# Two raw tiles for the rotary stage of a fused attention block, and a new order of the work around them

## The reference

```
x = x + attn(cond(x, subject, cond_weights, fside), WA, bA, WB, bB, WC, bC, WUQ, WUK, WUV, WZ, bZ)
x = x + ffn(lora(x, W, A, Bm, scalings, adapter), Wg, bg, W1, W2)

cond:  out = einsum('bct,bcd->bdt', x, cond_weights[subject]) + bias
attn:  h = x @ WA + bA;  kv_lat, q_lat = split(h)
       kRt = rope(h @ WB + bB)              # 64 rotary key features, shared by the heads
       qRt = rope(h @ WC + bC)              # 64 rotary query features for each of 16 heads
       q, k, v = q_lat @ WUQ, kv_lat @ WUK, kv_lat @ WUV
       scores = [q, qRt] . [k, kRt] / sqrt(192), causal;  softmax;  out = (attn @ v) @ WZ + bZ
rope:  x * cos + (pairs of x swapped, one of each negated) * sin
ffn:   4 experts, top 2, capacity 1024, gelu(x @ W1) @ W2, added to the tokens taken
```

## Time and profile before

| | |
|---|---|
| median of three runs | 1929.16 us |
| the profiled execution, its own time | 1927.72 us |
| its span, first to last instruction | 1925.6 us |
| mean granted TensorE clock | 0.985 |
| TensorE busy | 1825.1 us, 95% of the span |
| VectorE, ScalarE, GpSimd busy | 922.9, 627.2 and 705.7 us |
| attention's eight groups | about 46 to 967 us of the span |

### The profile page before, as it was taken

How to read it: one execution, slowest core, us unless ns; L and a number is a source line. 1 busy time by engine, 2 the same in 40 slices (tenths; PEclk the granted TensorE clock), 3 DMA queues, 4 the chain that set the end, 5 groups by cost and what they waited for, 6 DMA issues and landing times. The chain is left out here.

```text
span 1925.6 us, 29419 instructions
## 1 busy us (share of the span) xinstructions
PE 1825.1 (95%) x10664; PEld 1418.1 (74%) x10664; DVE 922.9 (48%) x1581; ACT 627.2 (33%) x1088; POOL 705.7 (37%) x525
## 2 busy tenths in 40 slices
PE   6899999999999999999999997999999999999996
PEld 4577676777767677677777776888888888888884
DVE  4565656556565665656433683242424232333321
ACT  4333333333333333333223112333333333333331
POOL 1232223223221222322100033565757575757563
PEclk9999999999999999999999998999999999999998
DMA  7000101010010100102033115033304230422011
GB/s 259 23 1 17 51 6 62 1 42 26 17 51 6 62 1 29 39 17 61 17 120 110 50 66 191 22 71 106 85 0 109 87 65 0 131 87 44 6 16 22
DMA packets 68588, 104.81 MB, mean 54 GB/s; under 512 B 12304, under 2 KB 29456, under 8 KB 68496
## 3 DMA queue, kind: packets, MB, share of 16 engines
q1 hardware_dynamic: 53568, 76.92, 12.2%
q0 software_dynamic: 7200, 16.78, 4.9%
q10 hardware_dynamic: 7728, 9.71, 1.4%
HBM read 78.23 MB, written 25.17 MB: 54 GB/s over the span
## 5 line engine op out<-in xcount | busy, mean ns | idle before, releaser
L1861 DVE CAST hh<-hid 128x512 fp32r<-128x512 f32 x128 | 92.6, 723 | 453.3 <-ACT hid L1806 453.3
L1731 POOL TENSOR_TENSOR w1l<-w_raw,w1h 128x512 fp32r<-128x512 f32 x112 | 185.3, 1654 | 153.4 <-ACT w1h L1798 153.3
L441 POOL TENSOR_TENSOR prob<-prob,rinv 128x512 f32<-128x512 f32 x64 | 66.7, 1043 | 460.1 <-DVE rinv L700 460.1
L95 PE MATMUL bank_o<-Mh,mix_h 128*128 128x512 f32 x512 | 211.6, 413 | 2.3 <-DVE mix_l L671 1.4
L95 PE MATMUL e_h<-xh,w1h 128*128 (+1 forms) x512 | 203.5, 397 | 5.6 <-POOL w1l L1731 5.6
L97 PE MATMUL e_h<-xh,w1l 128*128 (+1 forms) x512 | 202.7, 396 | 0.0
L96 PE MATMUL e_h<-xl,w1h 128*128 (+1 forms) x512 | 202.7, 396 | 0.0
L97 PE MATMUL bank_o<-Mh,mix_l 128*128 128x512 f32 x512 | 202.6, 396 | 0.0
L96 PE MATMUL bank_o<-Ml,mix_h 128*128 128x512 f32 x512 | 202.2, 395 | 0.0
L95 PE MATMUL e_y<-w2h,hh 128*128 128x512 f32 x512 | 201.2, 393 | 0.0
L96 PE MATMUL e_y<-w2l,hh 128*128 128x512 f32 x512 | 200.6, 392 | 0.0
(11 more groups left out here) (303 smaller groups left out, 3486.3 us busy)
## 6 DMA issues: line engine op xcount, KB each, us to landing
w_raw<-in_W_dram SPq DMA_DIRECT2D x56, 512.0 KB, 4.2
stage<-in_x_dram SPq DMA_DIRECT2D x8, 1024.0 KB, 6.3
x_res<-in_x_dram SPq DMA_DIRECT2D x32, 256.0 KB, 3.2
out_dram<-x_res SPq DMA_DIRECT2D x32, 256.0 KB, 2.0
flat_dram<-flat_sb ACTq DMA_DIRECT2D x32, 256.0 KB, 2.0
rows<-out_dram SPq DMA_DIRECT2D x4, 1024.0 KB, 5.4
stage<-in_W_dram SPq DMA_DIRECT2D x8, 512.0 KB, 5.6
x_res<-out_dram SPq DMA_DIRECT2D x3, 1024.0 KB, 5.2
```

What stands on the lines that cost most here:

```text
L95: nc.tensor.matmul(out, ah, bh, start=start and n == 0, stop=False)
L441: nc.gpsimd.tensor_tensor(prob[:, i % 2, :, :], prob[:, i % 2, :, :], rinv[:, :].unsqueeze(2).to_broadcast([P, HB, C]), ALU.mult).then_inc ...
L1731: nc.gpsimd.tensor_tensor(w1l[:, k, :, :], w1_at(pair, chunk), w1h[:, k, :, :].bitcast(F32), ALU.subtract).then_inc(S["w1_lo"], 1)
L1861: nc.vector.tensor_copy(hh[:, k, :], hid[:, k, :]).then_inc(S["h_hi"], 1)
```

## The change

`rope_raw` becomes two tiles used in turn: the keys take tile 0, query rotation u takes tile (u + 1) mod 2, and `q_raw` waits for the swap and the cosine product of the rotation before the last. On ScalarE, `prob_transposed(g, 1)` goes ahead of `exps(g, 2)`, the first `q_raw` of the second half ahead of `exps(g, 3)`, and `latent_bias(g + 1)` behind `prob_transposed(g, 5)`. On GpSimd all four cosine products of the second half go ahead of `gated(g, 3)` and `residual_bias(g, 1)`. On VectorE the second half's rotations move ahead: 5 ahead of `softmax_sum(g, 3)`, 7 ahead of `x2_tile(g, 0)`; and the first of four `spread` calls joins the other three behind them. TensorE's list is the same.

```
-        raw, swapped = sb("rope_raw", [P, GT]), sb("rope_swapped", [P, GT])
-        lat_bias = (raw, swapped)
+        raw, swapped = sb("rope_raw", [P, 2, GT]), sb("rope_swapped", [P, GT])
+        lat_bias = (raw[:, 0, :], swapped)
...
             def q_raw(g, u):
                 act.wait_ge(S["qr_mm"], g * NU + u + 1)
-                act.wait_ge(S["swap_ev"], g * NR + u + 1)
-                act.wait_ge(S["cos_ev"], g * NR + u + 1)
-                nc.scalar.activation(raw[:, :], bank_p[u % 2][:, :], ...
+                if u:
+                    act.wait_ge(S["swap_ev"], g * NR + u)
+                    act.wait_ge(S["cos_ev"], g * NR + u)
+                nc.scalar.activation(raw[:, (u + 1) % 2, :], bank_p[u % 2][:, :], ...
...
             def body(g, more):          # ScalarE
                 prob_transposed(g, 0)
                 mix_hi(g, 0)
-                exps(g, 2)
-
                 prob_transposed(g, 1)
+                exps(g, 2)
                 mix_hi(g, 1)
+                q_raw(g, UB)
                 exps(g, 3)
-                for u in range(UB, NU):
+                for u in range(UB + 1, NU):
                     q_raw(g, u)
...
                 exps(g, 6)
+                prob_transposed(g, 5)
                 if more:
                     latent_bias(g + 1)
-                prob_transposed(g, 5)
                 mix_hi(g, 5)
```

More of the change, by code:

```diff
@@ L426, in keys_cos @@
                 nc.gpsimd.tensor_tensor(k_rope[:, :].rearrange("p (b t) -> p b t", b=GB),
-                                        raw[:, :].rearrange("p (b t) -> p b t", b=GB),
+                                        raw[:, 0, :].rearrange("p (b t) -> p b t", b=GB),
                                         K.parts["cosk"].unsqueeze(1).to_broadcast([P, GB, C]),
@@ L434, in q_cos @@
                 nc.gpsimd.tensor_tensor(q_rope[:, u % UB, :].rearrange("p (b t) -> p b t", b=GB),
-                                        raw[:, :].rearrange("p (b t) -> p b t", b=GB),
+                                        raw[:, (u + 1) % 2, :].rearrange("p (b t) -> p b t", b=GB),
                                         cos.unsqueeze(1).to_broadcast([P, GB, C]), ALU.mult).then_inc(S["cos_ev"], 1)
@@ L463, in body @@
                 residual_bias(g, 0)
-                q_cos(g, 4)
-                q_cos(g, 5)
+                for u in range(UB, NU):
+                    q_cos(g, u)
                 gated(g, 3)
                 residual_bias(g, 1)
-                q_cos(g, 6)
-                q_cos(g, 7)
                 residual_bias(g, 2)
@@ L509, in keys_raw @@
                 act.wait_ge(S["keys_mm"], g + 1)
-                nc.scalar.activation(raw[:, :], bank_p[1][:, :], ACT.Identity, bias=K["bB"][:, 0:1]
+                nc.scalar.activation(raw[:, 0, :], bank_p[1][:, :], ACT.Identity, bias=K["bB"][:, 0:1]
                                      ).then_inc(S["raw_ev"], 1)
@@ L514, in q_raw @@
                 act.wait_ge(S["qr_mm"], g * NU + u + 1)
-                act.wait_ge(S["swap_ev"], g * NR + u + 1)
-                act.wait_ge(S["cos_ev"], g * NR + u + 1)
-                nc.scalar.activation(raw[:, :], bank_p[u % 2][:, :], ACT.Identity, bias=K["bC"][:, u:u + 1]
+                if u:
+                    act.wait_ge(S["swap_ev"], g * NR + u)
+                    act.wait_ge(S["cos_ev"], g * NR + u)
+                nc.scalar.activation(raw[:, (u + 1) % 2, :], bank_p[u % 2][:, :], ACT.Identity, bias=K["bC"][:, u:u + 1]
                                      ).then_inc(S["raw_ev"], 1)
@@ L558, in body @@
                 mix_hi(g, 0)
+                prob_transposed(g, 1)
                 exps(g, 2)
-                prob_transposed(g, 1)
                 mix_hi(g, 1)
+                q_raw(g, UB)
                 exps(g, 3)
-                for u in range(UB, NU):
+                for u in range(UB + 1, NU):
                     q_raw(g, u)
@@ L638, in latent_lo, with turn @@
                                         ALU.subtract).then_inc(S["lat_lo"], 1)
-            def turn(r, sin):
+            def turn(r, k, sin):
                 dve.wait_ge(S["raw_ev"], r + 1)
@@ L644, in turn @@
                 nc.vector.memset(wait_here[:, :], 0.0)
-                nc.vector.stream_shuffle(swapped[:, :], raw[:, :], [i ^ 1 for i in range(32)]
+                nc.vector.stream_shuffle(swapped[:, :], raw[:, k, :], [i ^ 1 for i in range(32)]
                                          ).then_inc(S["swap_ev"], 1)
@@ L655, in keys_rope @@
                 dve.wait_ge(S["lat_ev"], g * 2 + 2)
-                turn(r, K.parts["sink"])
+                turn(r, 0, K.parts["sink"])
                 dve.wait_ge(S["cos_ev"], r + 1)
@@ L662, in queries_rope @@
                 r = g * NR + 1 + u
-                turn(r, K.parts["sinq"][:, u * C:(u + 1) * C])
+                turn(r, (u + 1) % 2, K.parts["sinq"][:, u * C:(u + 1) * C])
                 dve.wait_ge(S["cos_ev"], r + 1)
@@ L735, in body @@
                 softmax_sum(g, 2)
-                if more:
-                    spread(g + 1, 0)
                 less_max(g, 3)
@@ L741, in body @@
                 queries_rope(g, 4)
+                queries_rope(g, 5)
                 softmax_sum(g, 3)
-                queries_rope(g, 5)
                 queries_rope(g, 6)
+                queries_rope(g, 7)
                 x2_tile(g, 0)
-                queries_rope(g, 7)
                 mix_lo(g, 2)
                 if more:
-                    spread(g + 1, 1)
-                    spread(g + 1, 2)
-                    spread(g + 1, 3)
+                    for i in range(NPAIR):
+                        spread(g + 1, i)
                 x2_tile(g, 1)
```

## The result

The changed kernel took 1915.16 us in the median of four runs (1910.64 to 1915.54), the kernel before 1929.11 us beside it (1926.45 to 1935.68). The ratio is 0.9916, with a 95% interval of 0.9898 to 0.9934: 0.84% faster. The forecast was 1945 us, slower, with a range of 1922 to 1956: wrong in its sign and outside the range.

The account below looks back on a forecast made before the run. It took TensorE, busy 95% of the span, as the bound, so only its waits could change. Terms summed to +7.1 us, +16.1 with the clock, on the profiled 1927.7; the median is 1.4 higher: 1945 us, range 1922 to 1956.

Parts of the forecast that it names:

- the schedule of the second half: VectorE's and GpSimd's rotations 4 to 7 in group 1's times: `x2_tile(0)` ends at 229.45, TensorE waits 4.1 us.
- the stand-in: Rotation 4's start on VectorE, taken from the last group before: 892.66 less 677.88, which is 214.78.
- The five collisions: Second half: VectorE's sine products and additions of rotations 4 to 7 held up by GpSimd; without collisions TensorE gains 1.5 us.
- The second half: `wz(g, 0)` 2.1 us later in groups 0 to 6, +3.8 us in the last group: +18.5 us together.
- The first half: `wz(6, 0)` starts at 292.3 instead of 293.52, 1.2 us won, seven times: -8.2 us.
- the bound that was stated: First half: 0 if GpSimd gets the port ahead of rotation 1's addition; the other end is -11.2 us.
- the border: First half: the worse rival takes over where rotation 1's addition starts after 290.95.
- Group 0's first half: Waits of 0.78 and 1.45 us there: -0.5 us, between 0 and -2.2.
- `latent_bias`: Behind `prob_transposed(5)` on ScalarE it takes away TensorE's 0.4 us wait for `probT`, 7 times: -2.7 us.
- The clock: A low-clock stretch behind each of eight 4.1 us waits, less two already there: +9 us, between -3 and +10.
- rival D: Worse: the first half's tie also goes to GpSimd, low stretches cost their whole 1.7 us: 1955 us, chance 0.10.
- B: Rival: `bank_o` is not late, VectorE gets through the four rotations without GpSimd in the way: 1900 us, chance 0.10.

Follow-up runs that it names:

- e_pause: The changed kernel with an unused VectorE maximum over 320 numbers, 0.41 us a group, ahead of rotation 4: 1957.4 us, 1.0143 of the kernel before.
- e_latent_back: The changed kernel with `latent_bias(g + 1)` back ahead of `prob_transposed(g, 5)` on ScalarE: 1917.13 us, 0.9932 of the kernel before.
- e_first: The changed kernel with `x2_tile(g, 5)` moved between the sine product and the addition of rotation 1: 1900.03 us, 0.984 of the kernel before.
- e_both_pause: The changed kernel with `x2_tile(g, 0)` ahead of rotation 7, `x2_tile(g, 5)` inside rotation 1, and a 320-number VectorE pause ahead of rotation 4: 1916.18 us, 0.9921.

## Why the prediction was wrong

The step that failed is in the schedule of the second half: "Rotation 4: shuffle to 215.5, sine to 216.3. GpSimd starts cosine 5 at 216.25, when the sine has let go". In before's times (3.55 us later by the reciprocals, 210.36 and 206.81), the shuffle started at 214.62 where I had 214.78, the sine ended at 216.08, the addition started at 216.11 and cosine 5 came at 216.32. Most likely the 0.16 us come from the stand-in, though no row prints a wait: in the last group before, the shuffle at 892.66 followed right behind ScalarE's writing of tile 4, which the change moves forward and which my own schedule had done by 213.4:

```profile
891.95 0.67 ACT L517 ACTIVATE rope_raw<-bank_p,bC 128x512 f32<-128x512 f32 x1
```
From the reciprocal to that shuffle it was 4.42 us there; in the kernel after it is 4.26, in group 1 and in the last group. Even from 214.78 the kernel's own steps lead VectorE's addition to 216.27, 0.05 us ahead of the cosine. I had a tie of a few hundredths between two engines on one lock, by estimates of 0.03 to 0.15 us for gaps, and decided it for GpSimd without naming it a tie; in the first half I did name one. The five collisions, each "like one that the rows show", hung on this one turn: with VectorE ahead, the cosines fall under shuffles and the sum, which take no turn. A reading was wrong too, without effect on the sum: the wait of 0.95 us stands at 451.64, in group 3 and not 4.

That VectorE and GpSimd take turns, whole instructions at a time, stood, and with it the schedule behind the lost turn: `e_pause` measures 4.31 us of wait for the forecast's 4.1. The Trainium skill (SBUF — State Buffer, "SBUF: two separate sides") says that whichever starts first holds the pair for its whole instruction. The traces agree, as when the cosine starts at 218.56 and the addition at 218.73 takes 1.67 us; what neither the rule nor I had was which one starts first.

Term by term, against the sum of the prediction:
- The second half, +18.5: measured -1.2 in group 1, and the last group 0.3 the other way: `wz(1, 0)` 15.13 us behind its rotation 4's first matmul (889.18 - 874.05), 14.80 before (903.62 - 888.82). Group 3, whose old wait was only 0.95, won 0.2. At group 1's figure for the other six that is -7.1 in all. This is the miss, some 26 us.
- The first half, -8.2: about 0, the bound that was stated. The keys' addition was blocked as foreseen (279.75, 1.67 us), but rotation 1's addition lost the turn to cosine 3 by 0.03 us (285.71 and 285.68; in before's times, 5.23 us later by the keys' first matmul, 290.94 and 290.91, just short of the 290.95 that I had named as the border). From the keys' first matmul block to `wz(6, 0)` it is 12.77 us, 12.80 before.
- Group 0's first half, -0.5: nothing; its two waits are the 2.1 us that are left for `rope_raw`.
- `latent_bias`, -2.7: right, by the waits that are gone and that `e_latent_back` brings back.
- The clock, +9: about -3.4. From one second half to the next it was 114.3 to 114.8 us before where a low stretch lay in between (groups 0, 2 and 4) and 112.9 in groups 1 and 5; after, 112.7 with the one at 648 (group 4) and 111.0 to 111.6 in groups 0 to 3 and 5. So a stretch costs between 1.1 and 1.9 us; at 1.7, three less one make -3.4. That a wait of 4 us brings a low stretch each time held in `e_pause`.

Together -7.1 - 2.7 - 3.4 = -13.2. From the first second half to the last the trace gives 792.7 us before (888.82 - 96.10) and 778.2 after (874.05 - 95.82), -14.5; the medians differ by 14.0. The rest, some 1 us, is within the spread of a stretch's cost.

`e_pause` also shows what the forecast would have been worth with the turn lost: 1957 us, above its 1945, since the first half gave nothing either, and nine low stretches of some 1.7 us came where it had eight of 1.5. That is the rival D. And B, at 0.10, had the right side for a wrong reason: not that GpSimd isn't in the way, but that it came second.

`e_first` won some 14 us by its ratio, where 1.53 us in seven first halves are 10.7. Its profiled execution is 11.6 us shorter than that of the kernel after (1901.1 and 1912.7): 10.4 less waiting for `x_res` (8.7 against 19.1) and no low stretch in the loop instead of one. What the ratio has beyond that is within the intervals.

## What to carry to other kernels

Where two engines share a lock, look for the one place at which the order is decided, write down the lead there, and when it is smaller than the estimates that it is made of, treat both outcomes as cases with a chance each; what follows is mostly one or the other, not a mean. Prefer an order in which the engine with idle time comes second: GpSimd lost 0.3 us a cosine and TensorE didn't wait for it, VectorE lost 1 us a product and TensorE waited 4. And take what the bound engine waits for (here `x2_tile`) off the end of the contended chain: that was worth as much again as the whole change.

## What the runs showed of the hardware

Whoever starts first keeps the port, down to leads of about 0.01 us. In the fourteen traces an addition of a rotation and a cosine product start within 0.1 us of each other 108 times. The cosine was first in 65, by 0.006 us or more, and the addition then took 1.79 to 1.84 us. The addition was first in 43, by 0.015 us or more, and took 0.69. Closer than that the recorded starts don't tell: in `e_both_pause` a sine product 0.002 us behind a cosine, at 325.77, kept its 0.69.

The loss is not symmetric, because the second one waits for the rest of the first: 128x512 additions on VectorE took up to 1.84 us instead of 0.69 behind a cosine, cosines up to 1.83 instead of 1.30 behind an addition. A start near the end of the other cost nothing: cosine 6 of the kernel after began at 215.53, in an addition that ran from 215.00 to 215.69, and took its 1.30. A delay of 0.41 us a group on one engine changed the run by some 44 us.
